# Moving set-up work inside the first attention stage, and the value folding inside the first feed-forward stage, of a gated cross-attention kernel

## What is computed

```
x = x + jnp.tanh(g_xattn[0]) * _L0_xattn_ref(_layernorm(x, axis=-1), ctx_1024)
x = x + jnp.tanh(g_ffn[0]) * _L0_ffn_ref(_layernorm(x, axis=-1), L0_ffn_w_gate, L0_ffn_w_up, L0_ffn_w_down)

def _L0_xattn_ref(query, values):
    scores = jnp.einsum('bqd,bkd->bqk', query, values)
    weights = jax.nn.softmax(scores, axis=-1)
    return jnp.einsum('bqk,bkd->bqd', weights, values)

def _L0_ffn_ref(x, w_gate, w_up, w_down):      # fp4_linear quantises both its inputs in blocks of 16
    gate = fp4_linear(x, w_gate)
    y = fp4_linear(x, w_up)
    h = jax.nn.silu(gate) * y
    return fp4_linear(h, w_down)
```

## Time and profile before

| | |
|---|---|
| median of 3 runs | 1145.91 us (1144.83 to 1147.27) |
| profiled execution, its own time | 1137.96 us |
| span of the profiled execution | 1136.2 us |
| first stage, first product to last copy | 8.76 to 103.11 us |
| FFN 0, to the first transposes of the next stage | 103.11 to 280.65 us |

### The profile page before, as it was taken

The page is one execution under the profiler, slowest core; times in us unless marked ns, Lnnn a source line. Parts: engine busy times, 40 slices in busy tenths (PEclk is TensorE's granted clock), DMA queues, the critical chain, the costliest instruction groups (busy, mean ns, idle before and its releaser), DMA issues.

```text
span 1136.2 us, 18807 instructions
## 1 busy us (share of the span) xinstructions
PE 1057.8 (93%) x6234; PEld 901.9 (79%) x6234; DVE 794.2 (70%) x1816; ACT 517.3 (46%) x1191; POOL 164.2 (14%) x227
## 2 busy tenths in 40 slices
PE   4875799998999989998999997999989999999998
PEld 3754477776899968887888886999958888888887
DVE  5877899976788756537888875888647564565554
ACT  2565544442555545554544552565643333333322
POOL 2231000000112043211111101033323010010000
PEclk9988899999999979999999999999989999999999
DMA  9401010000100000000000004100012121121220
GB/s 286 96 1 40 1 11 1 1 1 27 49 1 0 1 12 1 1 1 1 1 1 0 1 1 174 64 0 1 1 53 70 59 72 59 57 82 39 74 83 29
DMA packets 30374, 41.19 MB, mean 36 GB/s; under 512 B 13615, under 2 KB 19577, under 8 KB 29414
## 3 DMA queue, kind: packets, MB, share of 16 engines
q1 hardware_dynamic: 29437, 39.63, 11.0%
q10 hardware_dynamic: 873, 0.72, 0.3%
HBM read 37.80 MB, written 2.54 MB: 36 GB/s over the span
## 4 chain that ended last, share of the span: by engine, by line
PE 50%; DVE 2%; ACT 1%; DMA 0%; issue 0%; POOL 0%; POOLq 0%; DVEq 0%; SPq 0%; ACTq 0%
PE psum L1958 16%; PE psum L1969 8%; PE psum L1362 6%; PE psum L1340 5%; PE psum L1177 3%; PE psum L1135 2%; PE psum L349 2%; PE psum L1350 2%; PE psum L1159 1%; PE psum L1148 1%; PE psum L1379 1%; PE psum L1930 1%; PE psum L854 0%; PE psum L1920 0%; DMA work<-expert_shares 0%
## 5 line engine op out<-in xcount | busy, mean ns | idle before, releaser
L298 POOL TENSOR_TENSOR rstd<-ve,mhalf 128x1 f32<-128x1 f32 x128 | 81.9, 641 | 713.1 <-DVE ve L293 713.1
L360 ACT COPY work<-psum 128x256 f32<-128x256 f32 (+1 forms) x240 | 99.1, 437 | 146.4 <-PE psum L349 141.3
L349 PE MATMUL psum<-ident,work 128*128 128x128 f32 (+1 forms) x624 | 101.6, 285 | 29.9 <-DMA ctx<-in_ctx_r 8.8
L349 PEld LDWEIGHTS psum<-ident,work 128*128 128x128 f32 (+1 forms) x624 | 76.3, 148 | 45.8 <-DMA ctx<-in_ctx_r 8.8
L2043 ACT CAST h_hi<-work 128x512 fp32r<-128x512 f32 x68 | 42.2, 621 | 122.1 <-DVE work L2113 95.9
L2103 DVE TENSOR_TENSOR work<-psum,work 128x512 f32<-128x512 f32 x68 | 46.9, 690 | 72.3 <-ACT work L2035 72.1
L1555 PE MATMUL psum<-early,work 128*128 128x352 f32 x256 | 83.1, 480 | 6.7 <-ACT zone L493 4.0
L1958 PE MATMUL psum<-x_hi,ew_hi 128*128 128x512 f32 (+1 forms) x272 | 86.2, 398 | 0.2 <-ACT work L2035 0.2
L1958 PE MATMUL psum<-x_hi,ew_lo 128*128 128x512 f32 (+1 forms) x272 | 84.0, 390 | 0.0
L1958 PE MATMUL psum<-x_lo,ew_hi 128*128 128x512 f32 (+1 forms) x272 | 84.0, 390 | 0.0
L1969 PE MATMUL psum<-ew_hi,h_hi 128*128 128x256 f32 x272 | 76.2, 280 | 2.6 <-DVE h_lo L2120 2.5
(11 more groups left out here) (263 smaller groups left out, 2547.9 us busy)
## 6 DMA issues: line engine op xcount, KB each, us to landing
work<-expert_shares SPq DMA_DIRECT2D x64, 256.0 KB, 3.2
early<-in_experts_in SPq DMA_DIRECT2D x1, 6528.0 KB, 18.9
x<-in_x_in SPq DMA_DIRECT2D x4, 512.0 KB, 7.3
early<-in_W_in SPq DMA_DIRECT2D x2, 1024.0 KB, 5.9
out_x<-x SPq DMA_DIRECT2D x3, 512.0 KB, 4.4
early<-in_Wk SPq DMA_DIRECT2D x1, 1024.0 KB, 6.7
early<-in_Wq SPq DMA_DIRECT2D x1, 1024.0 KB, 8.8
zone<-in_Wv SPq DMA_DIRECT2D x1, 1024.0 KB, 14.1
```

The costliest lines, as they stand in the source:

```text
L298: pool.tensor_tensor(rstd[:, slot:slot + 1], ve[:, slot:slot + 1], mhalf[:, 0:1], ALU.pow).then_inc(s["rstd_ready"], 1)
L349: last = pe.transpose(dst[0:rows, at:at + n], src, ident[0:n, 0:n])
L360: act.copy(dst, src).then_inc(s["tr_copied"], 1)
```

## The change

1. In the first stage TensorE calls `setup_units(t)` in front of the values product instead of behind it.
2. The query column moves from step 7 to step 6, and ScalarE scales one half of Wq in step 6 and the other in step 7.
3. The key split of layer 1 is made in four parts of 616 columns: ScalarE's in steps 8 to 11, VectorE's in steps 10 to 13.
4. The gate of the first attention is multiplied into the context (one ScalarE instruction before the pipeline), and VectorE's L1034 falls away.
5. In FFN 0 the folding starts at the beginning: four units in step -2, two in step -1, then one in each of steps 0 to 13. In step -2 ScalarE copies the normalised rows before its other work.

```
-        VO_FIRST, VO_UNITS = 4, 2
+        VO_RAMP = {-2: 4, -1: 2}
+        VO_LAST = B * KT - sum(VO_RAMP.values())
...
-            return VO_UNITS if not isinstance(t, int) or 0 <= t - VO_FIRST < B * KT // VO_UNITS else 0
+            return VO_RAMP.get(t, 0) if isinstance(t, int) and t < 0 else int(not isinstance(t, int) or t < VO_LAST)
...
+        def key_split_scalar(act, l, cols=slice(0, B * HK)):
+            act.copy(kb_hi[l][:, cols], kb_raw[l][:, cols]).then_inc(set_s["kb_hi_done"], 1)
+
+        def key_split_vector(dve, l, n):
+            cols = key_part(n)
+            dve.wait_ge(set_s["kb_hi_done"], n + 1)
...
-                if t == 7:
+                if t == 6:
                     pe.wait_ge(ld["wq2"], 16 * 3)
                     pe.wait_ge(set_s["prep"], 2)
                     unit(query_column)
...
+                setup_units(t)
                 if has(t - 1):
                     pe.wait_ge(s["tr_copied"], pt_unit)
                     wait(pe, s["y_read"], t - 2)
+                    if t == 1:
+                        pe.wait_ge(q_s["tables"], 2)
                     c = ((t - 1) // TB) * (D + 1)
                     pe.matmul(bank[6 + p][:, 0:D + 1], prT0, ctx1[:, c:c + D + 1],
                               start=True, stop=True).then_inc(s["y_ready"], 1)
-                setup_units(t)
...
-                if t == 8:
-                    act.wait_ge(set_s["read"], un.n)
-                    key_split_scalar(act, 1)
+                if 8 <= t < 8 + KEY_PARTS:
+                    if t == 8:
+                        act.wait_ge(set_s["read"], un.n)
+                    key_split_scalar(act, 1, key_part(t - 8))
...
+            act.wait_ge(q_s["tables"], 1)
+            act.wait_ge(ld["ctx"], 16 * 3)
+            gated = ctx1[:].rearrange("p (b d) -> p b d", b=B)[:, :, 0:D]
+            act.activation(gated, gated, ACT.Identity, scale=tg[0:SK, 0:1]).then_inc(q_s["tables"], 1)
...
-                    link(dve, dve.tensor_tensor(small[:, 3:4], small[:, 2:3], tg[:, 0:1], ALU.mult))
-                    dve.scalar_tensor_tensor(xt(t - 2), y[:, 0:D], small[:, 3:4], xt(t - 2), ALU.mult,
+                    dve.scalar_tensor_tensor(xt(t - 2), y[:, 0:D], small[:, 2:3], xt(t - 2), ALU.mult,
...
+                if t in (-4, -3):
+                    take_fold(-2, (2 * t + 8, 2 * t + 9))
```

More of the change, by code:

```diff
@@ L547, in take_wide_values @@
             return last
-        VO_FIRST, VO_UNITS = 4, 2
+        VO_RAMP = {-2: 4, -1: 2}
+        VO_LAST = B * KT - sum(VO_RAMP.values())
         def vo_unit(t, i):
-            n = VO_UNITS * (t - VO_FIRST) + i
+            n = i + sum(vo_units(u) for u in range(-2, t))
             return n // KT, n % KT
         def vo_units(t):
-            return VO_UNITS if not isinstance(t, int) or 0 <= t - VO_FIRST < B * KT // VO_UNITS else 0
+            return VO_RAMP.get(t, 0) if isinstance(t, int) and t < 0 else int(not isinstance(t, int) or t < VO_LAST)
         def fold_values(pe, dst, bb, k):
@@ L760, in bias_vector @@
         def bias_vector(dve):
[L761 removed]
+            dve.wait_ge(q_s["tables"], 3)
             dve.wait_ge(set_s["filled"], GATE_UP_UNITS)
@@ L958, in setup_units @@
                         unit(take_wide_keys, j)
-                if t == 7:
+                if t == 6:
                     unit(lambda act, src: act.copy(b["qcol"], src[:, 0:8]))
                     act.wait_ge(set_s["read"], un.n)
-                    for k in range(KD):
-                        act.activation(b["Wq"][:, k, :], b["Wq"][:, k, :], ACT.Identity,
-                                       scale=b["gsc"][:, k:k + 1]).then_inc(set_s["wq_scaled"], 1)
+                if t in (6, 7):
+                    k = t - 6
+                    act.activation(b["Wq"][:, k, :], b["Wq"][:, k, :], ACT.Identity,
+                                   scale=b["gsc"][:, k:k + 1]).then_inc(set_s["wq_scaled"], 1)
                 if t in (8, 9, 10):
@@ L1045, in start_vector @@
                     prepare_queries(dve)
-                if t == 10:
-                    key_split_vector(dve, 1)
+                if 10 <= t < 10 + KEY_PARTS:
+                    key_split_vector(dve, 1, t - 10)
                 if t == 13:
@@ L1535, in ffn0_tensor, with fold @@
             s, tr = f_s[0], Count()
+            def fold(t):
+                for i in range(vo_units(t)):
+                    wait(pe, s["tr_copied"], tr.n - 1)
+                    fold_values(pe, bank[TR45[tr.odd]], *vo_unit(t, i)).then_inc(s["tr_filled"], 1)
+                    tr.up()
             def step(t, p):
@@ L1565, in step @@
                     last.then_inc(s["y_ready"], 1)
+                if t == -2:
+                    fold(t)
                 if has(t + 2):
@@ L1577, in step @@
                     tr.up()
[L1578 to L1581, removed]
+                if t != -2:
+                    fold(t)
             pipeline(pe, -2, step, (), T + 1)
@@ L1587, in ffn0_scalar, with take_fold @@
             s, tr = f_s[0], Count()
+            def take_fold(t, units):
+                for i in units:
+                    src = bank[TR45[tr.odd]]
+                    act.wait_ge(s["tr_filled"], tr.up())
+                    take_folded_values(act, src, *vo_unit(t, i)).then_inc(s["tr_copied"], 1)
             def step(t, p):
+                if t == -2:
+                    take(act, s, tr, xnT[p], P, D, TR45, KD)
                 if has(t - 2):
@@ L1607, in step @@
                                    scale=rstd[:, slot:slot + 1]).then_inc(s["xn_ready"], 1)
-                if has(t + 2):
+                if t in (-4, -3):
+                    take_fold(-2, (2 * t + 8, 2 * t + 9))
+                if has(t + 2) and t != -2:
                     take(act, s, tr, xnT[p], P, D, TR45, KD)
@@ L1618, in step @@
                     key_split_scalar(act, 3)
[L1619 to L1622, removed]
+                if t != -2:
+                    take_fold(t, range(vo_units(t)))
             pipeline(act, -4, step, (), T + 1)
@@ L1679, in step @@
                                              ALU.mult, ALU.mult).then_inc(s["nmr_ready"], 1)
-            pipeline(dve, -5, step, [(tr, 6 + 2 * VO_UNITS), (chain_n, 2 * (4 + 2 + 2))], T + 2, 5)
+            pipeline(dve, -5, step, [(tr, 6 + 2), (chain_n, 2 * (4 + 2 + 2))], T + 2, 5)
             end_stage(dve, "dve")
```

18 lines of the change are left out of this document (7 added, 11 removed).

## The result

The changed kernel takes 0.9912 of the time before, with a 95% interval of 0.9892 to 0.9932 (median 1131.55 against 1144.8 us, 20 runs each). On the 1145.91 us from which the prediction started, that is 10.1 us less, between 7.8 and 12.4; predicted were 10.4. The two medians by themselves lie 13.3 us apart and the two means 11.2, because both kernels scatter (1137.7 to 1147.3 us before, 1126.0 to 1141.0 changed); the ratio with its interval is what the text goes by. Measured a second time beside the last experiments it was 0.9924 (0.9893 to 0.9954). The profiled execution took 1130.14 us.

A forecast was written before the change was run, and what follows sets the result against it. TensorE was taken to bound FFN 0, and waits between engines the first stage. First stage -5.4 and FFN 0 -5.0 gave -10.4 us, from 1145.91 to 1135.5 us; the 8-in-10 range was 1129.5 to 1142.

The forecast's parts named there:

- the rival with the larger gain: Wait behind the query column stays small (1130.8 us), or the key cast's cost goes too (1128.5 us); chance 0.14.
- L1034 and the key parts: First stage: fourteen L1034 instructions gone from VectorE's steps, -2.8 us; its key split in four parts, +0.4 us.
- the first rival: First stage: VectorE waits 0.6 us more in steps 5 to 12, for values products or locked ports; 1140.3 us, chance 0.14.
- The new wait for y(5): First stage, step 7: VectorE waits 3.7 us for the values product behind the query column, 1.0 for scores; +4.7 us.
- Half of the 1.0 is the clock: First stage: half the 1.0 us wait for tile 8's scores comes from TensorE's clock falling behind the query column.
- The old waits, -7.2: First stage: VectorE's waits of 3.8 us for ScalarE's copies and 3.4 us for scores fall away, -7.2 us.
- The four small waits, +1.0: First stage: late values products in steps 5, 8, 11 and late quantisation in step 12, 0.3 us each; +1.0 us.
- The pauses at the end, -1.5: First stage's end, behind VectorE's last step: a values-product pause of 1.32 us and two of 0.1 go, -1.5 us.
- Fold products, -7.3: FFN 0, steps 4 to 13: 17 fold products instead of 34, at 0.43 us each, -7.3 us.
- the 9.69 us that the prediction took for VectorE's own step: FFN 0: VectorE's step of 9.69 us against TensorE's 9.27; VectorE takes back at most half a microsecond.
- The key cast, +2.3: FFN 0, step 2: ScalarE's layer 3 key cast stands before the fold's copy, delaying tile 5's gate and up; +2.3 us.
- Everything later keeps its instructions.: Behind FFN 0: the instructions stay the same, and the sum has no term for this stretch.

The follow-up runs named there:

- the two parts alone: Kernel before with only the FFN 0 part of the change: 0.9953; with only the first-stage part: 0.9995, repeated 0.9978.
- order alone: Kernel before with one edit, TensorE calling the set-up units in front of the values product: 0.9986 of before.
- order undone: Changed kernel with the values product again in front of the set-up units, all else as changed: 0.9912 of before.
- the kernel of the last experiment: Changed kernel with query column in three units, layer 3 key cast behind the fold's copy, ScalarE's first two step-8 copies before its quantisation: 0.9851 of before.
- the short column: Changed kernel with 15 of the query column's 16 products left out, so its output is not the reference's: 0.9884 of before.
- the cut column: Changed kernel with the query column in three units, each with its own scaling of Wq, and the key cast behind the fold's copy: 0.9886 of before.

## Why the prediction was right, and which of its terms were not

The sum was right, 10.4 us for 10.1 measured (7.8 to 12.4); so were its halves in the pair of profiles (-4.9 for -5.4, -4.9 for -5.0). Over all profiles the first stage gives -5.0 (103.7 to 98.7) and FFN 0 -6.9 (178.5 to 171.6, five each with the cast in front). That the pair agrees better than these means is partly luck, and so is how close the ratio came: by the medians alone the gain would have been 13.3, near the 15.1 of the rival with the larger gain. In timed runs the two parts alone add up to 6.9 us with about 4 either way, so the runs bear out the sum and not its split. Term by term:

- **L1034 and the key parts, -2.8 and +0.4.** Right. Without L1034 VectorE's list is 2.5 us shorter from tile 2's row maximum to tile 15's (13 of them). The key parts took 0.98, 0.79, 0.80 and 0.79 us and overlap a little with what follows: from start to start 3.03 us for 2.63. None was held long by GpSimd, as the first rival feared.
- **The new wait for y(5), the values product of tile 5, +4.7.** The mechanism was right. In the four other profiles of the changed first stage, where the column took 3.70 us, it was 3.64 to 3.69 for the values product and 0.37 to 0.72 for the scores, 4.1 to 4.4 in all. In the profiled execution it was 6.0, with the column itself at 4.78 us for 3.70. "Half of the 1.0 is the clock" put the fall behind the column; that time it came inside.
- **The old waits, -7.2.** Right as a total, wrong in part as to cause. They did not all stand in steps 9 and 10: 0.81 us of the 3.4 for scores stood in step 6, ahead of the column. Part of them was not the column, the scaling or the cast but the place of the units behind the values product: order alone and order undone put 2.5 and 2.9 us on it, by one profile each and not by the timed runs. The prediction gave the order no price in the steps.
- **The four small waits, +1.0.** Beside the column's, VectorE waited 1.1 us for TensorE and ScalarE up to tile 15 in the two profiles whose clock was 1.00 from 58 to 63 us, and 2.8 in the three with 0.50 there. All these waits together came to 6.7 us on the mean of the five, for 8.3 on the mean of the three old ones: -1.6, where -7.2 + 4.7 + 1.0 gives -1.5. In the pair itself it was only -0.3 (7.4 to 7.1); there the rest came from gaps that the prediction had no term for.
- **The pauses at the end, -1.5.** Mis-sized. From VectorE's last step to the last copy it was 12.04 us before and 10.76 after (87.47 to 98.23), but 11.6 to 12.2 in the other four profiles with the changed first stage: -0.4 on the mean. The clock goes with it: the 10.76 had 1.00 from 88 to 93 us, the other four had 0.86 (11.85), 0.73 (11.61) and 0.50 twice (12.14 and 12.22). At 1.00 the three old ones had 12.04 to 12.23, and the changed kernel with the order undone 11.87. So at the full clock the order gains 1.1 to 1.5 us here, near the forecast, and beside a low clock most of it is gone. No run changes the clock alone, so that stays a reading of nine profiles.
- **Fold products, -7.3.** It was -8.0: 120.20 to 112.22 us from tile 5 on, and within 0.03 of the one or the other in every profile. A product costs 0.47 and not 0.43 us (3.29 us for the seven in the gap; the difference of two rows had made it too small). VectorE did not become the bound: from tile 5 to tile 15 TensorE took 92.01 us, 9.20 a step, and VectorE kept up. So the 9.69 us that the prediction took for VectorE's own step were not its limit.
- **The key cast, +2.3.** Mis-sized: the pause itself is 1.6. Counted from the stage's start, tile 5 came 3.1 us later in the pair, 1.1 on the mean of five profiles each: where the low clock falls in the stage's first steps moves it by as much as the cast does.
- **"Everything later keeps its instructions."** True, and its time still moved: by +1.9 us in the pair, by up to 12.5 between any two executions. The span of one profile is no check on a sum of this size; the prediction's range allowed for it, but its text did not say it.

None of the rivals came about. The values product made VectorE wait three times in the profiled execution (five in the second profile), not in every step. FFN 0 gave its part alone (0.9953). The rival with the larger gain, the wait behind the column gone, was the kernel of the last experiment, and it needed two more edits than it named. Open are how little of the first stage's gain the timed runs show where its part stands alone, and the order's share in them.

## What to carry to other kernels

A long unit that is moved or cut does not give back its length: ask what stood in its shadow, and remove that in the same step (by one profile each, the short column won 3.2 of 4.6 us, the cut column nothing until ScalarE's two copies were moved as well). On an engine that serves two others, put what someone waits for ahead of what has to wait for its own input. Where a kernel's clock wanders, compare stages over several profiles and kernels that share the stage's code, and trust a single one only where it runs at the full clock.

## What the runs showed of the hardware that I had not expected

- The same instructions met the low clock at different places from execution to execution. The 32 matmul records of the query column took 3.70 us in one and 4.78 in another, with the same work ahead of them.
- What lies behind FFN 0 took 854.5 to 867.0 us over fourteen executions, though not one instruction of it differs between the kernels: 1.5% of that stretch, more than the whole change is worth.
- A pause of TensorE of 2.47 us was followed by about 15 us at the low clock, and with the pause cut to 0.69 us the clock stayed up in the same place. The pause of 3.39 us with the short column was followed by a low clock too (0.50 from 53 to 58 us). Each of these is one profile. In the best kernel the column's first two parts (12 records each, 1.5 us) had the full clock on both sides.
- The Trainium skill, "TensorE: Matmul & The Clock Gate", section "What's actually happening", says that activity releases the half rate, the default. The pair with and without the pause agrees with that. The fall inside the whole column, with TensorE busy by the profile in 4.84 of the 5 us around it, does not follow from it as it stands.
